# Two-layer attention and FFN kernel: the PSUM banks split four and three instead of three and four

## The reference

```python
# layer 0
x = x + _L0_xattn_ref(_layernorm(x), ctx_512, ...)   # causal self attention plus cross attention to 512 context rows
x = x + _L0_ffn_ref(_layernorm(x), w1, b1, w2, b2)   # quantized 256 -> 1024 -> 256, GELU
# layer 1
x = x + _L1_xattn_ref(_layernorm(x), ctx_512, ctx_512, ...)   # cross attention, softmax over 512 context rows
x = x + _L1_ffn_ref(_layernorm(x), w1, b1, w2, b2)   # quantized with one scale for the whole tensor, GELU

# each attention
scores = jnp.einsum('bhqd,bhkd->bhqk', qh, kh) * scale
attn = jax.nn.softmax(scores, axis=-1)
out = jnp.einsum('bhqk,bhkd->bhqd', attn, vh)
```

## Time and profile before

| | |
|---|---|
| median of 3 runs | 1774.21 us (1771.69 to 1776.6) |
| the profiled execution | 1775.95 us |
| its span, first to last instruction | 1774.2 us |
| busy: PE, DVE, ACT, POOL | 1550.6, 1325.8, 1133.0, 464.8 us |
| mean granted TensorE clock | 0.916 |

### The profile page before, as it was taken

How to read it: one execution, slowest core, us unless ns; L and a number is a source line. 1 busy time by engine, 2 the same in 40 slices (tenths; PEclk the granted TensorE clock), 3 DMA queues, 4 the chain that set the end, 5 groups by cost and what they waited for, 6 DMA issues and landing times.

```text
span 1774.2 us, 31229 instructions
## 1 busy us (share of the span) xinstructions
PE 1550.6 (87%) x11094; PEld 664.0 (37%) x11094; DVE 1325.8 (75%) x2583; ACT 1133.0 (64%) x2178; POOL 464.8 (26%) x677
## 2 busy tenths in 40 slices
PE   3998889988998989988998989998988997888677
PEld 1344335423442334323542335323543442232226
DVE  5787766788678777887687866878578687788287
ACT  1374576566756686666665775667655854866497
POOL 3211413330323122421333122421342222310130
PEclk8788979998999989998998989989998898899898
DMA  6322201212121212121121212121121011011313
GB/s 184 94 83 91 87 19 44 70 45 66 35 76 46 63 43 64 52 76 42 38 77 35 61 43 64 52 75 49 58 64 37 27 55 40 25 56 42 143 60 120
DMA packets 115018, 110.99 MB, mean 63 GB/s; under 512 B 21552, under 2 KB 108720, under 8 KB 114864
## 3 DMA queue, kind: packets, MB, share of 16 engines
q1 hardware_dynamic: 114864, 108.99, 20.6%
HBM read 69.35 MB, written 38.80 MB: 61 GB/s over the span
## 4 chain that ended last, share of the span: by engine, by line
PE 55%; DVE 19%; ACT 13%; issue 5%; POOL 3%; DMA 2%; SPq 2%; ACTq 0%; POOLq 0%; DVEq 0%
PE acc L1633 14%; PE st L1619 10%; DVE nmax L1372 9%; PE misc L1563 8%; PE misc L1535 6%; PE misc L1589 5%; ACT probs L1053 5%; PE misc L1660 3%; PE misc L1575 3%; ACT tail_h L1123 2%; DMA stack<-nrow 2%; PE misc L1600 2%; PE misc L1687 2%; ACT tail_h L1108 1%; DVE hid L1321 1%
## 5 line engine op out<-in xcount | busy, mean ns | idle before, releaser
L1372 DVE TENSOR_REDUCE nmax<-misc 128x1 f32<-128x512 f32 (+3 forms) x1408 | 856.4, 658 | 250.1 <-PE misc L1600 127.3
L1053 ACT ACTIVATE probs<-st 128x512 f32<-128x512 f32 (+3 forms) x1536 | 742.6, 548 | 316.6 <-PE st L1619 213.6
L1619 PE MATMUL st<-stack 50*128 50x512 f16 (+3 forms) x1536 | 458.0, 377 | 68.5 <-ACT probs L1053 54.6
L1589 PE MATMUL misc<-stack 48*128 48x512 f16 (+3 forms) x1536 | 483.2, 377 | 38.6 <-DVE nmax L1372 30.8
L1619 PEld LDWEIGHTS st<-stack 50*128 50x128 f16 x1536 | 110.9, 95 | 460.2 <-ACT probs L1053 263.2
L1633 PE MATMUL acc<-probs,v_x 128*32 128x512 f32 x1152 | 178.5, 696 | 0.0
L1589 PEld LDWEIGHTS misc<-stack 48*128 48x128 f16 x1536 | 125.8, 95 | 110.9 <-DVE nmax L1372 82.2
L1039 ACT ACTIVATE qk<-misc,b 128x512 f32<-128x512 f32 x96 | 65.9, 687 | 149.8 <-PE misc L1563 149.6
L932 POOL TENSOR_TENSOR parts<-qk,zero 128x512 f16<-128x512 f32 x78 | 81.1, 1040 | 297.6 <-ACT qk L1039 297.5
L1633 PE MATMUL acc<-probs,v_s 128*32 128x512 f32 (+3 forms) x1152 | 117.7, 482 | 0.1
L1633 PE MATMUL acc<-probs,v_f 128*32 128x512 f32 x768 | 111.3, 654 | 0.0
(11 more groups left out here) (282 smaller groups left out, 2090.9 us busy)
## 6 DMA issues: line engine op xcount, KB each, us to landing
parts_xk<-parts SPq DMA_DIRECT2D x36, 128.0 KB
parts_xq<-parts SPq DMA_DIRECT2D x36, 128.0 KB
stack<-parts_xq SPq DMA_DIRECT2D x72, 64.0 KB, 2.1
stack<-parts_xk SPq DMA_DIRECT2D x72, 64.0 KB, 2.1
xn_A<-in_x_dram SPq DMA_DIRECT2D x8, 512.0 KB, 4.3
hid<-in_L_ffn_w_dram SPq DMA_DIRECT2D x4, 1024.0 KB, 5.4
parts_sk<-parts SPq DMA_DIRECT2D x32, 128.0 KB
parts_sq<-parts SPq DMA_DIRECT2D x32, 128.0 KB
```

The source lines that it names most:

```text
L1053: act.activation(probs[:, j % P_SLOTS, c, T - w:], st_bank(n, 4 * j + c)[:, 0:w], ACT.Exp, scale=scale_of[s.unit[1]]).then_inc(exp_done, 1)
L1372: dve.tensor_reduce(nmax[:, ring, first:first + NT * (len(cs) - 1) + 1:NT], src, AX.X, ALU.max, negate=True).then_inc(misc_free[slot], 1)
L1589: last = pe.matmul(o, stack[rows, r, 0, c // 2, P * i:P * i + P], stack[rows, r, 1, c // 2, 0:w], start=True, stop=not causal)
L1619: last = pe.matmul(o[:, 0:w], stack[rows, r, 1, c // 2, P * j:P * j + P], stack[rows, r, 0, c // 2, T - w:T], start=True, stop=not causal)
```

## The change

One bank goes from the ring `misc` to the ring `st`: scores rotate through four banks, maxima and all other uses through three. Everything that follows from the two constants (`st_bank`, `misc_slot`, the waits and the head start) moves with them. In the tail the banks named by hand are named anew, as `misc[3]` does not exist any more: `turn_banks` takes `misc[2]` for `st[2]`, the third pair of `up_pairs` is `st[2:4]` for `misc[2:4]`, and the two banks of the peak are `st[2]` and `st[3]` for `misc[2]` and `misc[3]`.

```diff
-ST_BANKS, MISC_BANKS, P_SLOTS, QK_RING = 3, 4, 2, 4
+ST_BANKS, MISC_BANKS, P_SLOTS, QK_RING = 4, 3, 2, 4
...
-        turn_banks = [st[2], acc]
-        up_pairs = [st_all[:, 0:2, :], misc_all[:, 0:2, :], misc_all[:, 2:4, :]]
+        turn_banks = [misc[2], acc]
+        up_pairs = [st_all[:, 0:2, :], misc_all[:, 0:2, :], st_all[:, 2:4, :]]
...
-            dve.tensor_reduce(trow[:, 1:2], misc[2][0:1, 0:P], AX.X, ALU.max).then_inc(t_row, 1)
+            dve.tensor_reduce(trow[:, 1:2], st[2][0:1, 0:P], AX.X, ALU.max).then_inc(t_row, 1)
...
-            dve.tensor_scalar(hscale[:, :], misc[3][:, 0:1], 1e-6, 1.0 / QP, ALU.max, ALU.mult).then_inc(t_hsc, 1)
+            dve.tensor_scalar(hscale[:, :], st[3][:, 0:1], 1e-6, 1.0 / QP, ALU.max, ALU.mult).then_inc(t_hsc, 1)
...
-            pe.transpose(misc[2][0:1, 0:P], hrun1[:, :], ident[:, :]).then_inc(t_htot, 1)
+            pe.transpose(st[2][0:1, 0:P], hrun1[:, :], ident[:, :]).then_inc(t_htot, 1)
...
-            to_all(misc[3][:, 0:1], trow[:, 1:2]).then_inc(t_htot, 1)
+            to_all(st[3][:, 0:1], trow[:, 1:2]).then_inc(t_htot, 1)
```

## The result

The changed kernel takes 1829.38 us (1825.03 to 1831.87, four runs) against 1772.95 (1769.56 to 1776.6, four runs) for the kernel before: a ratio of 1.0318, with an interval of 1.0291 to 1.0346. That is 56 us slower where I forecast 16: the right side, inside the range, and 40 us off. The profiled execution took 1831.87 us, its span 1830.1. I read the same views as before, in the same order.

A forecast was written before the change was run, and what follows sets the result against it. No engine is full; the coupling of TensorE, VectorE and ScalarE bounds the loop. The terms, -18 + 11 + 23 = +16 us, take 1775.95 to 1792 (1790 on the median's scale), with a range of 1750 to 1842.

The forecast's parts named there:

- Term 1: Groups with fewer than four maxima: the fourth score no longer waits for its own group's first exponential; 18 us gained.
- Term 2: The other 109 groups: the fourth maximum waits for its group's first reduction, 0.10 us later than the exponential; 11 us lost.
- Term 3: Where VectorE lags, `misc` banks are released one read later: 35 x 0.658 = 23 us lost, upper bound 88.
- Other users of `misc`: Projections, transposes and the hidden layer meet the same kind of delay as maxima; left inside the 88 us upper bound.
- Faster: The score ring was the real limit and the maxima's ring has slack: -32 us, 1744; chance 0.27.
- No difference: The wait only moves; VectorE's reductions set the group's length under either split: 1776, within 5 us; chance 0.13.
- Much slower by lag: Every waiting weight load of a maximum counts, +88 us: +81 in sum, 1857; chance 0.14 together with the clock case.
- By the clock: Idle gaps between matmuls lower the clock in all eight turns: 32 us more, 1824; chance 0.14 together with lag.
- the 0.02 named as a sign: The forecast is wrong if the granted clock of the turns moves by more than 0.02 either way.

The follow-up runs named there:

- e1: Kernel before with three banks for scores and three for `misc`, the eighth bank unused in the loop: 1845.72 us, 1.0403.
- e5: Kernel before with one of the four `misc` banks kept for the fourth maxima of full units, all else on a ring of three: 1807.4 us, 1.0198.
- e12: Kernel before with one of the four `misc` banks kept for turned heads and turned maxima, all else on a ring of three: 1804.6 us, 1.02.

## Why the prediction was off

**Term 1 had the right size, half of it in the wrong place.** It forecast 18 us gained; the fourth score bank brings 16 (e1 against the changed kernel). The sign named for it came too: the array's idle time before a score fell to 6.9 us, below the 20 that I had set. But the term looked for the gain in groups with fewer than four maxima. Measured group by group between e1 and the changed kernel, 8.0 us of it lie in the 20 groups without maxima (that at 1648.28 took 2.45 us, now 1.72), nothing in the 129 with one to three, and 9.8 us in the 224 with four, where the term had none. So the number is in part luck. The count under it was off as well: by the rule as stated the trace has 202 groups and not 161, of which 127 have four or more maxima (not 109) and 75 fewer (not 52). With these the terms are -20, +13 and +23, and the sum stays at +16.

**Term 2 was right at the places that it rested on.** The group at 592 grew by 0.06 us, as worked out. That at 521 grew by 0.19 where I had 0.14. As a count it was too narrow, by the same error as term 3: it charged the fourth maximum alone.

**Term 3 is the step that failed.** Together with term 2 it put the lost `misc` bank at 34 us; e1 shows 72. The bank is released one read later, as the term said: the 155 waits added take 0.59 us on average, near the 0.658 us of a read. The failure is the number of places. I took the array's own waits, 35, "because a weight load that waits under a running matmul costs nothing". The runs show many more places, 155 more waiting loads, and most of the added time not at the fourth maximum but at the second and third (14.1 us, now 71.3), since a small use of the ring beside the maxima moves the shortage forward. From all rows of matmuls and weight loads I worked out how much of the loads' waits for VectorE and ScalarE lay under a running matmul: 356 of 514 us before, 437 of 609 after, so 81 of the 95 us added. That these waits are free does not hold. In the profiled executions the durations of all matmuls add up to the same (4452 us and 4447, with 13 matmuls missing from the second record), but they overlap by 50 us less, and so the array's busy time grew by 45 us and its idle time by 11; that is the whole 56. The profile models the ends of matmuls, so the overlap is as good as that model. The reading that fits is that after a late load the next matmul starts on its own, where otherwise it would have run beside the one under way, and everything queued behind it comes later by as much. That each late load costs overlap is argued from these sums and not shown. Nor do the waits of the loads give the size: they lay at 88 us in my upper bound, near the 72, but e5 and e12 show that the time does not follow them.

The second half of the same error: I looked for places only where something already waited. In the group at 515.32 nothing did, and it lost 0.59 us, the turned maxima taking a bank that the ring of four had to spare. "Other users of `misc`" I had left inside the upper bound; e12 shows that 192 of them are worth 41 us.

**The signs.** Weight loads waiting for reductions rose by 155 times (about a hundred forecast); the array's idle time before a maximum doubled, as forecast (30.8 to 59.5); VectorE's share of the chain grew and ScalarE's shrank, as forecast. Those signs were right with a sum that was off by more than twice, so they test the mechanism and not its size. Of the 155, 95 are at the fourth maxima of groups with four, as forecast, but these hold only 26 of the 91 us added.

**The rivals.** *Faster* rested on the 115 waits against 35; it decided on whether the fourth maximum mostly finds its bank free, and it does not: 137 of the 224 wait. *No difference* holds in single groups like that at 592; but over the 60 groups with four maxima and nothing else the change is +9.8 us. *Much slower by lag* (1857) charged every load that already waited; the result lies between it and the forecast, but the time went to other places than those loads. *By the clock* is not seen: 0.917 after 0.916, and the turn at 0.96 in both kernels is 8 us longer. Single turns did move by more than the 0.02 named as a sign, both ways: that from 222 us from 0.94 to 0.91, that from 1002 us from 0.91 to 0.96. The Trainium skill, TensorE: Matmul & The Clock Gate, "A second HAM failure mode: psum-queue depth-cycling", has short idle times between groups that cycle through banks as a cause of lower clock; here the array's idle time grew only from 223.5 to 234.3 us, and the mean clock did not move.

The rule of the Trainium skill (Perfetto Trace Analysis, "Optimizing Tensor Performance", Matmuls), cited ahead of the result, that matmul groups should rotate through banks, holds for both rings: each gained from one bank more. It doesn't say which ring should have the bank; in the runs the gain from the one (16) is far below the loss from the other (72).

## What to carry to other kernels

When a buffer moves from one ring to another, count for both rings how many buffers a repeating piece of the program asks for, with every small user in the ring, and charge each piece in which the demand exceeds the smaller ring, also those in which nothing waits today. Don't size the loss by the idle time of the engine alone: here a wait that lay under work came back as less overlap, in the busy time. The waits of the instruction that needs the buffer first (here the weight load) show where the buffers are short, but not how much that costs. To size it, run the kernel with the buffer taken from one ring and given to none; that one run separates the gain from the loss.

## What the runs showed of the hardware that I had not expected

- The array's busy time rose by 45 us with the same matmuls of the same summed duration, as they overlap less. That late weight loads are the reason is argued above. A busy time is not the work done.
- Scores and maxima of other heads start within 60 ns of each other 906 times and run together; with an order that leaves 202 of these the kernel is 22 us slower (1.0111).
- A maximum put off by one product costs 92 us (1921.53 against 1829.38), more than the bank that it was to save. Why it is so dear was not settled.
